# First sequence's features in two halves of tokens, and another order of the loads, in a four-sequence transformer block kernel

## What is computed

```python
h = relu(x @ (down_project * dg + db)) @ (up_project * ug + ub) + x     # dg, db, ug, ub from the condition
paths = sigmoid(h @ Wp + bp)                                            # 8 heads of depth 5
agree = pq * pk + (1 - pq) * (1 - pk)
sim   = cumprod(agree).sum() / 5                                        # causal mask, softmax
x = x + (softmax(sim) @ (h @ Wv)) @ Wo
U = (condition @ W_dec + b_dec)                                         # 257 x 30 for each sequence
y = x @ (U[:-1] @ V) + U[-1] @ V
x = x + y + y @ expert_w[argmax(y @ gate_w)]
```

## Time and profile before

| | us |
|---|---|
| median of 3 runs | 155.72 (155.0 to 155.99) |
| profiled execution, its own time | 155.55 |
| its span | 153.4 |
| PE busy in the span | 141.2 (92%) |
| DVE busy | 83.7 (55%) |
| ACT busy | 58.8 (38%) |
| POOL busy | 31.2 (20%) |

### The profile page before, as it was taken

One profiled execution on the slowest core, in us unless ns is written; L12 is line 12 of the kernel. 1 busy time (PEld: TensorE's weight loads), 2 busy tenths in 40 slices (PEclk: granted clock), 3 DMA queues, 4 the chain that ended last, 5 costly groups with the idle time before them and its releaser, 6 DMA issues.

```text
span 153.4 us, 5078 instructions
## 1 busy us (share of the span) xinstructions
PE 141.2 (92%) x2296; PEld 89.8 (59%) x2296; DVE 83.7 (55%) x156; ACT 58.8 (38%) x70; POOL 31.2 (20%) x56
## 2 busy tenths in 40 slices
PE   5989678999497999999999999999999999999992
PEld 5746155554274777457656655567558577666650
DVE  0563532619966378296915483558146851985431
ACT  3013156264226342558333451573434447310010
POOL 7200004100405302640022205200222440110000
PEclk9999999999999999999999999999999999999999
DMA  4989999600011200000101000100011010110112
GB/s 121 311 320 433 448 376 353 209 4 0 0 22 17 35 0 4 0 4 0 37 3 38 34 4 0 38 0 4 34 38 38 0 38 0 38 38 34 68 38 71
DMA packets 7381, 12.50 MB, mean 81 GB/s; under 512 B 1552, under 2 KB 5808, under 8 KB 7232
## 3 DMA queue, kind: packets, MB, share of 16 engines
q10 hardware_dynamic: 2496, 7.23, 12.1%
q1 hardware_dynamic: 4768, 4.89, 9.9%
q0 software_dynamic: 96, 0.05, 1.1%
HBM read 9.95 MB, written 2.22 MB: 79 GB/s over the span
## 4 chain that ended last, share of the span: by engine, by line
PE 83%; DVE 11%; ACT 2%; issue 1%; POOL 0%; ACTq 0%; POOLq 0%; DVEq 0%
PE work L561 36%; PE c_ps L561 24%; PE s_ps L561 17%; PE work L738 3%; DVE rden L420 2%; DVE feat L552 2%; PE work L678 2%; DVE tiles L509 1%; ACT prob L365 1%; DVE h_t L455 1%; ACT phi_t L390 1%; DVE u_row L481 1%; PE work L730 1%; DVE x_t L541 1%; DVE logit L464 0%
## 5 line engine op out<-in xcount | busy, mean ns | idle before, releaser
L365 ACT ACTIVATE prob<-s_ps 128x1536 f32<-128x1536 f32 (+1 forms) x24 | 38.2, 1593 | 39.3 <-PE s_ps L561 36.3
L420 DVE RECIPROCAL rden<-c_ps 128x256 f32<-128x256 f32 x16 | 28.1, 1757 | 26.5 <-PE c_ps L561 26.5
L342 POOL TENSOR_SCALAR_AFFINE_SELECT prob<-prob 128x1024 f32<-128x1024 f32 x16 | 20.1, 1257 | 93.1 <-ACT prob L365 93.1
L561 PE MATMUL s_ps<-phi_t 32*128 32x256 f32 (+1 forms) x384 | 24.2, 365 | 1.6 <-ACT phi_t L390 1.0
L561 PE MATMUL c_ps<-prob,v_sb 128*32 128x256 f32 (+1 forms) x384 | 24.9, 346 | 0.0
L561 PEld LDWEIGHTS s_ps<-phi_t 32*128 32x128 f32 x384 | 17.4, 184 | 10.6 <-issue 6.8
L561 PE MATMUL work<-ctx_t,mix_sb 128*32 128x256 f32 x256 | 17.0, 381 | 0.4
L561 PE MATMUL work<-zo_t,gexp 128*32 128x256 f32 x256 | 16.9, 379 | 0.0
L561 PEld LDWEIGHTS c_ps<-prob,v_sb 128*32 128x32 f32 x384 | 11.5, 109 | 9.0 <-issue 2.0
L561 PE MATMUL c_ps<-prob,ones 128*32 128x256 f32 (+1 forms) x256 | 16.3, 326 | 0.0
L561 PE MATMUL work<-w_vl,h_t 128*32 128x296 f32 x208 | 14.8, 416 | 1.1 <-DVE h_t L455 0.6
(11 more groups left out here) (95 smaller groups left out, 133.4 us busy)
## 6 DMA issues: line engine op xcount, KB each, us to landing
wdec<-in_W_dec ACTq DMA_DIRECT2D x1, 3855.0 KB, 15.2
x_t<-in_x_tr SPq DMA_DIRECT2D x4, 512.0 KB, 9.3
ex_t<-in_expert_tr ACTq DMA_DIRECT2D x1, 2048.0 KB, 22.1
out_x<-x_t SPq DMA_DIRECT2D x16, 128.0 KB, 1.7
mix_sb<-in_mix ACTq DMA_DIRECT2D x1, 776.0 KB, 16.8
lift_sb<-in_lift ACTq DMA_DIRECT2D x1, 384.0 KB, 3.7
w_vl<-in_vl SPq DMA_DIRECT2D x1, 296.0 KB, 4.9
first_sb<-in_first SPq DMA_DIRECT2D x1, 144.0 KB, 3.5
```

What stands on the lines that cost most here:

```text
L342: nc.gpsimd.affine_select(out=tri, in_=tri, compare_op=ALU.is_ge, fill=0.0, base=0, pattern=[[0, HG], [0, 2], [1, P]], channel_multiplier= ...
L365: nc.scalar.activation(prob[:, p % 2, :, 0:width(p)], s_ps[:, :, 0:width(p)], ACT.Exp).then_inc(exped, 1)
L420: link(nc.vector.reciprocal(rden[:], c_ps[m % 2][:, CW:2 * CW]))
L561: return nc.tensor.matmul(o, w, r, start=start, stop=stop, skip_group_check=True)
```

## The change

- The chain bias, tanh, feat, phi of sequence 0 is done for tokens 0 to 255 (FIRST) and 256 to 511 (SECOND) apart. VL 2 and 3 of sequence 0 stand behind the first half's steps; scores 0 and 1 need the first half only. The second half of phi stands behind scores 1.
- phi_t of group 1 is written by DVE, no longer by ACT, for all sequences.
- gdn (1,2,3) stands where gup 1 stood and gup 1 behind the ups; its DVE work is two instructions of three sequences instead of six. gup 2 and gup 3 leave the prologue for the gaps behind context 0 and scores 6.
- VL and the features of sequence 1, the U steps, Q, and G 1 stand elsewhere in the gaps of sequence 0.
- x of sequence 0 comes in two halves over the queues of SyncE and ACT; wdec comes in two halves of partitions over the same two, issued at the start, ahead of x of sequence 2 and 3. All of ACT's loads are issued at the start. One warm-up matmul fewer.

```diff
-WARM = 9
+WARM = 8
...
-PROLOGUE = [("gdn", (0,)), ("gup", 0), ("down", 0), ("gup", 1), ("up", 0, 0), ("up", 0, 1), ("gdn", (1, 2, 3)),
-            ("VL", 0, 0), ("VL", 0, 1), ("VL", 0, 2), ("VL", 0, 3), ("bias", 0), ("tanh", 0), ("feat", 0),
-            ("gup", 2), ("gup", 3), ("phi", 0, 0), ("phi", 0, 1), ("scores", 0), ("down", 1)]
+def part(b, ts):
+    return 1 if ts == FIRST else b + 2
+def features(b, ts):
+    return [("bias", b, ts), ("tanh", b, ts), ("feat", b, ts)]
+PROLOGUE = [("gdn", (0,)), ("gup", 0), ("down", 0), ("gdn", (1, 2, 3)), ("up", 0, 0), ("up", 0, 1), ("gup", 1),
+            ("VL", 0, 0), ("VL", 0, 1), *features(0, FIRST), ("VL", 0, 2), ("VL", 0, 3), ("bias", 0, SECOND),
+            ("phi", 0, 0, FIRST), ("phi", 0, 1, FIRST), ("tanh", 0, SECOND), ("scores", 0), ("feat", 0, SECOND),
+            ("down", 1)]
...
     if b == 0:
-        gaps[1] += [("VL", n1, 2), ("VL", n1, 3)]
-        gaps[2] += [("U", 1)]
-        gaps[3] += [("U", 3)]
-        gaps[5] += [("G", 1), ("Uadd",)]
+        gaps[0] = [("phi", b, 0, SECOND), ("phi", b, 1, SECOND)] + gaps[0]
+        gaps[1] += [("U", 0)]
+        gaps[2] += [("VL", n1, 2), ("VL", n1, 3)] + features(n1, ALL_T)
+        gaps[3] += [("U", 2)]
+        gaps[5] += [("gup", 3), ("Uadd",)]
...
     if b == 0:
-        gaps[0] += [("VL", n1, 0), ("VL", n1, 1)]
-        gaps[1] += [("bias", n1), ("tanh", n1), ("U", 0), ("feat", n1)]
-        gaps[2] += [("U", 2)]
-        gaps[3] += [("Q",)]
+        gaps[0] += [("gup", n2)]
+        gaps[1] += [("VL", n1, 0), ("VL", n1, 1)]
+        gaps[2] += [("U", 1)]
+        gaps[3] += [("Q",), ("U", 3)]
         gaps[4] += [("G", 0), ("ubT",)]
-        gaps[5] += [("down", n2), ("WoU",)]
+        gaps[5] += [("G", 1), ("down", n2), ("WoU",)]
...
-        _k, _late = _late % 2, _late + 1
+        _k, _late = 1 - _late % 2, _late + 1
...
-            sp.dma_start(x_t[:, 0], x_tr[0].rearrange("(c p) t -> p c t", p=P)).then_inc(ld_x[0], 16)
+            sp.dma_start(x_t[:, 0, 0], x_tr[0, 0:P]).then_inc(ld_x[0], 16)
             sp.dma_start(w_vl[:], vl.rearrange("p (c n) -> p c n", c=DC)).then_inc(ld_vl, 16)
-            for b in range(1, B):
-                sp.dma_start(x_t[:, b], x_tr[b].rearrange("(c p) t -> p c t", p=P)).then_inc(ld_x[b], 16)
+            sp.dma_start(wdec[0:P // 2], W_dec[0:P // 2]).then_inc(ld_wdec, 16)
+            sp.dma_start(mix_sb[:], mix).then_inc(ld_mix, 16)
+            sp.dma_start(x_t[:, 2], x_tr[2].rearrange("(c p) t -> p c t", p=P)).then_inc(ld_x[2], 16)
...
+            act.dma_start(x_t[:, 0, 1], x_tr[0, P:2 * P]).then_inc(ld_x[0], 16)
             act.dma_start(lift_sb[:], lift).then_inc(ld_lift, 16)
+            act.dma_start(x_t[:, 1], x_tr[1].rearrange("(c p) t -> p c t", p=P)).then_inc(ld_x[1], 16)
+            act.dma_start(wdec[P // 2:P], W_dec[P // 2:P]).then_inc(ld_wdec, 16)
+            act.dma_start(ex_t[:], expert_tr.rearrange("e (c p) f -> p e c f", p=P)).then_inc(ld_ex, 16)
+            act.dma_start(x_t[:, 3], x_tr[3].rearrange("(c p) t -> p c t", p=P)).then_inc(ld_x[3], 16)
...
-                elif s[0] == "phi":
-                    _, b, g = s
+                elif s[0] == "phi" and s[2] == 0:
+                    _, b, g, ts = s
...
+                elif kind == "phi" and s[2] == 1:
+                    _, b, g, ts = s
+                    tok = slice(P * ts[0], P * (ts[-1] + 1))
+                    full(dve, s)
+                    nc.vector.tensor_scalar(phi_t[:, b % 2, g, tok], bank(s)[:, tok], rootc[:], None, op0=ALU.mult
+                                            ).then_inc(empty(s), 1)
...
                 if p % BP < NG:
-                    done(pe, ("phi", b, g))
+                    done(pe, ("phi", b, g, ALL_T if b else FIRST))
+                elif b == 0 and first:
+                    done(pe, ("phi", b, g, SECOND))
```

More of the change, by code:

```diff
@@ L76 @@
 ALL_T, FIRST, SECOND = (0, 1, 2, 3), (0, 1), (2, 3)
[L77 to L82 removed]
+def part(b, ts):
[6 more added lines that the diff above has]
+            ("down", 1)]
+EARLY_BANK = {("gdn", (0,)): 0, ("gup", 0): 1, ("down", 0): 2, ("gdn", (1, 2, 3)): 3, ("up", 0, 0): 4, ("up", 0, 1): 5,
+              ("gup", 1): 0, ("VL", 0, 0): 1, ("VL", 0, 1): 2, ("VL", 0, 2): 4, ("VL", 0, 3): 5,
+              ("phi", 0, 0, FIRST): 1, ("phi", 0, 1, FIRST): 2}
 def after_scores(b):
@@ L124, in after_context @@
     if b >= 1 and n1 < B:
-        gaps[2] += [("bias", n1), ("tanh", n1), ("feat", n1)]
+        gaps[2] += features(n1, ALL_T)
     if prv >= 1:
@@ L435, in _ @@
                     full(dve, s)
[L436 to L443, removed]
+                    bs, n = slice(s[1][0], s[1][-1] + 1), len(s[1])
+                    link(nc.vector.tensor_tensor(w_dn[:, bs], dproj[:].unsqueeze(1).broadcast_to([P, n, DC, HD]),
+                                                 g[:, bs, 0:HD].unsqueeze(2).broadcast_to([P, n, DC, HD]), ALU.mult))
+                    nc.vector.tensor_tensor(w_dn[:, bs], w_dn[:, bs],
+                                            g[:, bs, HD:2 * HD].unsqueeze(2).broadcast_to([P, n, DC, HD]), ALU.add
+                                            ).then_inc(empty(s), 1)
                 elif kind == "gup":
@@ L457, in _ @@
                 elif kind == "bias":
-                    b = s[1]
-                    if b == 0:
+                    _, b, ts = s
+                    span = slice(ts[0], ts[-1] + 1)
+                    if ts == FIRST:
                         dve.wait_ge(ld_bp, 16)
[L461 to L465, removed]
-                                            ).then_inc(logit_ready, 1)
+                    if b >= 1:
+                        dve.wait_ge(sign_ready, part(b, ts) - 1)
+                    done(dve, ("VL", b, ts[-1]))
+                    nc.vector.tensor_tensor(logit[:, span], v_sb[:, b % 2, span, D:],
+                                            bp_b[:].unsqueeze(1).broadcast_to([P, len(ts), H * DEPTH]), ALU.add
+                                            ).then_inc(logit_ready, 1)
+                elif kind == "phi" and s[2] == 1:
+                    _, b, g, ts = s
+                    tok = slice(P * ts[0], P * (ts[-1] + 1))
+                    full(dve, s)
+                    nc.vector.tensor_scalar(phi_t[:, b % 2, g, tok], bank(s)[:, tok], rootc[:], None, op0=ALU.mult
+                                            ).then_inc(empty(s), 1)
                 elif kind == "Q":
@@ L543, in _ @@
                 elif kind == "feat":
-                    b = s[1]
-                    dve.wait_ge(sign_ready, b + 1)
+                    _, b, ts = s
+                    rows = slice(H * ts[0], H * (ts[-1] + 1))
+                    dve.wait_ge(sign_ready, part(b, ts))
                     if b >= 1:
-                        full(dve, ("phi", b - 1, NG - 1))
-                    link(nc.vector.tensor_copy(feat[:, :, 1:2], sign[:, :, 0:1]))
+                        full(dve, ("phi", b - 1, NG - 1, SECOND if b == 1 else ALL_T))
+                    link(nc.vector.tensor_copy(feat[:, rows, 1:2], sign[:, rows, 0:1]))
                     for i in range(1, DEPTH):
                         n = 2 ** i
-                        ins = nc.vector.tensor_tensor(feat[:, :, n:2 * n], feat[:, :, 0:n],
-                                                      sign[:, :, i:i + 1].broadcast_to([P, TT * H, n]), ALU.mult)
+                        ins = nc.vector.tensor_tensor(feat[:, rows, n:2 * n], feat[:, rows, 0:n],
+                                                      sign[:, rows, i:i + 1].broadcast_to([P, H * len(ts), n]),
+                                                      ALU.mult)
                         if i < DEPTH - 1:
@@ L648, in _ @@
                         done(pe, ("gdn", (0,) if b == 0 else (1, 2, 3)))
-                    pe.wait_ge(ld_x[b], 16)
+                    pe.wait_ge(ld_x[b], 16 if b else 32)
                     for c in range(DC):
@@ L674, in _ @@
                 elif kind == "phi":
-                    _, b, g = s
-                    pe.wait_ge(feat_ready, b + 1)
-                    for t in range(TT):
+                    _, b, g, ts = s
+                    pe.wait_ge(feat_ready, part(b, ts))
+                    for t in ts:
                         ins = nc.tensor.transpose(
```

21 lines of the change are left out of this document (9 added, 12 removed).

## The result

The changed kernel took 186.16 us (median of four runs, 185.15 to 186.96) against 155.53 us for the kernel before in the same session: 1.197 times as long, with a 95% interval from 1.189 to 1.205. The forecast was 157.1, with a range from 154.4 to 158.5. The profiled execution took 186.96 us, its span 184.9.

A forecast was written before the change was run, and what follows sets the result against it. PE was taken as the bound, its early stalls deciding: +0.08 + 3.47 - 2.10 - 0.87 + 3.10 = 3.68 us ahead at context 3, becoming -1.46 at WoU. Thus 155.55 became 157.0, plus 0.17 for the median: 157.1, range 154.4 to 158.5.

The forecast's parts named there:

- Part 1: Start to the first VL matmul: practically nothing gained, VL at 11.58 us against 11.66 before.
- 157.0 of the sum: Whole kernel: the profiled 155.55 us before, plus the loss of 1.46 us at WoU, gives 157.0 us.
- Start of part 1: Loads up to down 0: x in halves gains nothing, lift lands about 5.8 us, down 0 starts at 7.00 as before.
- rival C: Start-up: the clock's fast rate may come later, slowing matmuls from 7.0 to 10 us; +1.5 us, 158.5; chance 0.06.
- Part 2: VL to the first scores: 6.18 us instead of 9.65, first scores at 17.76, 3.55 us earlier.
- Part 3: Scores 0 to first up of sequence 1: 5.47 us against 3.37, phi_t queued behind the second exponential; loss 2.1 us.
- Part 4: Up 1 to context 3: PE runs without a wait, gup 2 adds 0.87 us; context 3 at 38.77, 3.7 us ahead.
- Part 5: Context 3 to the last u_row: DVE's order takes 5.72 us, ending at 44.49, 0.9 us later than before.
- Part 6: Last u_row to WoU: DRAM trip 7.85 us, DVE queue 3.10; WoU at 55.44 against 53.98, PE idle 2.6 us.
- Later nothing gives it back: Behind WoU: PE is full, so the loss of 1.46 us at WoU stays to the end.
- Rival A: The trip through DRAM before WoU does not bind, so no loss: WoU at 53.75, time 155.5 us; chance 0.12.
- Rival B: Start-up loads (lift or bp) land late, each us passing to the end; 158.1 us at 1 us late; chance 0.2.

The follow-up runs named there:

- experiment 8: Three edits of e5_u3_ahead: one phi_t on VectorE, 153.06 us; x of sequence 0 over two queues, 155.15 us; that phi_t plus a ninth warm-up matmul, 152.88 us.
- e2_old_loads: The changed order of steps with the loads of the kernel before, each at its old engine and place; 159.77 us, ratio 1.022.
- e5_u3_ahead: e2_old_loads with U 3 ahead of context 3, G 1 (gexp 1) ahead of Uadd and gup 3 behind WoU; 153.98 us, ratio 0.989.
- e6_wdec_whole: e1_x3_on_sync with wdec as one undivided load on SyncE instead of two halves on two queues; 159.46 us over ten runs.
- e1_x3_on_sync: The changed kernel with x of sequence 3 issued by SyncE instead of ACT; 163.87 us, ratio 1.052.

## Why the prediction was wrong

It was wrong by 29 us, for one cause, and right in nearly every step that it had worked out.

- **Part 1 is the step that failed.** It priced what the new loads do to the DMA engines (lift at 5.8 us) and not what issuing them does to ScalarE. It took the ups to be filled 1.17 us behind gdn, that is, the Relu of act_t to run right behind down as before. In the program's order that Relu stood behind six issues. No row of before shows an issue that was held; there ex_t was the last of ScalarE's loads, with nothing behind it. Other unseen costs were bounded from both sides, this one was not bounded at all: its lower end is an issue of 0.5 us, its upper end the landing of what stands ahead in the queue. The issue came out at 30.19 us, and PE's wait for act_t at 26.1.
- **The sum of the loss.** act_t at 35.19 and not 8.14: 27.05 us. From there to the first scores 1.9 us more than forecast (46.70 against 17.76 + 27.05), with the clock at 0.50: the first up step took 2.08 us where the same eight matmuls took 1.14 at full clock. WoU to the end took 184.9 - 84.39 = 100.5 us, before 99.4: 1.1, with the clock at 0.63 from 85 to 88. Together 30.0; the profiled execution lay 30.0 above the 157.0 of the sum.
- **Start of part 1, x over two queues: right, for the loads.** The lift came in 0.2 us after PE asked for it, and experiment 8 shows the same zero by itself. But down 0 started at 7.68, not at 7.00: the two gup matmuls took 1.73 us and not 1.05, though the granted clock reads 1.00. They took 1.72 in `e2_old_loads` and 1.13 in `e5_u3_ahead`, which have the loads of before and the same eight warm-up matmuls, so it differs from run to run. That is what rival C named, at 0.7 us or less; the stall hid it in the kernel after.
- **Part 2: right.** `e2_old_loads` took 6.15 us from VL to scores, forecast 6.18.
- **Part 3: right.** 5.38 us in both kernels, forecast 5.47, with PE waiting 1.3 us for ScalarE's phi_t. Experiment 8 took that wait away and got 0.94 us of it back.
- **Part 4: right,** 15.44 us in `e2_old_loads` (15.54). **Part 5: right,** 5.67 (5.72).
- **Part 6: right in both terms.** After the last u_row u_raw was in 8.2 us later (7.85) in the kernel after, and from there to WoU it took 2.98 us (3.10). PE waited 3.07 and 2.86 us (2.6).
- **"Later nothing gives it back": true, but something can take more.** The wait of 2.9 us ahead of WoU was counted at its length, and the clock that fell behind it cost `e2_old_loads` some 2 to 3 us more. In the profiled run of `e6_wdec_whole` the same wait cost no more than its length. The prediction had the clock among its rivals (C), but at the start-up.
- **Rival A** did not come true: in `e2_old_loads` the trip and the queue behind it held WoU for 2.9 us. Its condition was then made: with u_row 2.1 us earlier and gexp ahead of Uadd the trip no longer holds WoU (`e5_u3_ahead`). It stood at 155.5; the measured 153.98 shows that, the queue on DVE mended, more was to be had.
- **Rival B** named the right place, the loads at the start, and the wrong mechanism: bp landed after 10.6 us and lift after 4.7, neither late enough to matter. Its price of about 1 us per microsecond of delay holds roughly; the delay was 27 and the loss 30. A second cost, x of sequence 1 behind the rows of wdec (2.3 us in `e1_x3_on_sync`), nobody had named.

So the change of order is worth 1 to 2% once its two new waits are removed, and the change of loads turned it into a loss of 20%.

## What to carry to other kernels

An engine that computes should not issue a load behind others of many rows that are still on their way in its queue; here up to 1,344 rows issued ahead did no harm and 1,600 did. The price of such an issue is not 0.5 us: in all four cases it lasted at most until what stood ahead had landed, and it falls on whatever the engine computes next. A load moved to the start must be followed on its issuing engine as well as on the DMA engines. A wait of PE of 1.3 us or more in this kernel may also bring the clock down behind it, in some runs and not in others, so count it at its length or more, and remove such waits first.

## What the runs showed of the hardware

- An issue on ScalarE's queue took 0.34 to 0.85 us, or 14.26, 20.76, 28.43 and 30.19 us with enough outstanding ahead of it (and 3.80 for the one behind that of 20.76); in three of these four cases it ended when the transfer ahead of ex_t had landed, within 0.9 us, in the fourth 6.4 us earlier. Rows issued ahead fit as what is counted (1,344 taken, 1,600 held), the number of transfers and their bytes do not; it was not tested by itself.
- Two halves of 64 partitions moved at 209 to 214 GB/s with the DMA engines at 0.92 to 1.00 of their time, one transfer of 128 partitions at 398 to 417.
- The granted clock stood at 0.50 for about 6.8 us around the end of a wait of 2.9 us in a stretch where PE was half busy (profiled run of `e2_old_loads`), and for at least 2 us after a wait of 1.3 us (`e5_u3_ahead`). It stayed at 1.00 with the same two waits in the profiled run of `e6_wdec_whole`, and in the kernel before with a wait of 2.2 us. From run to run the same program had mean clocks of 0.946 to 1.00 (`e6_wdec_whole`).
